# Plain fp32 products for every up-projection of a scan and mixture-of-experts kernel, in place of some products of high and low fp32r parts

## What is computed

```python
state = state * dA + (d_t * u_t)[..., None] * B_t[:, None, :]
y_t = jnp.einsum('ben,bn->be', state, C_t)
...
shared_out = jax.nn.silu(xf @ shared_wg.T) * (xf @ shared_wu.T) @ shared_wd.T
h = jax.nn.silu(jnp.einsum('td,efd->etf', xf, exp_wg)) * jnp.einsum('td,efd->etf', xf, exp_wu)
all_out = jnp.einsum('etf,edf->etd', h, exp_wd)
```

## Time and profile before

| | |
|---|---|
| median of 3 runs | 253.39 us (253.25 to 253.78) |
| the profiled execution's own time | 253.55 us |
| its span (first to last instruction) | 251.7 us |
| mean granted TensorE clock, share of full speed | 0.919 |
| matmul records on PE | 874 |

### The profile page before, as it was taken

One profiled execution on the slowest core, in us unless ns is written; L12 is line 12 of the kernel. 1 busy time (PEld: TensorE's weight loads), 2 busy tenths in 40 slices (PEclk: granted clock), 3 DMA queues, 4 the chain that ended last, 5 costly groups with the idle time before them and its releaser, 6 DMA issues. The chain is left out here.

```text
span 251.7 us, 3757 instructions
## 1 busy us (share of the span) xinstructions
PE 205.5 (82%) x874; PEld 148.7 (59%) x874; DVE 215.0 (85%) x522; ACT 171.2 (68%) x508; POOL 195.3 (78%) x237
## 2 busy tenths in 40 slices
PE   8534594658669895677996899889999999999995
PEld 4223273434355662345854587568888778788884
DVE  2789999999998989999999999989999999645340
ACT  4579879997758997458757998676775682343220
POOL 0248889999999999999999999999999996510000
PEclk9855579575979999999999999999999999999999
DMA  6496999770490202002209302020300000000000
GB/s 183 140 263 172 336 410 321 281 230 1 130 364 12 83 21 87 0 16 68 81 14 329 109 0 83 27 83 3 101 3 0 22 3 3 21 0 0 3 21 21
DMA packets 26821, 25.45 MB, mean 101 GB/s; under 512 B 1064, under 2 KB 25904, under 8 KB 26160
## 3 DMA queue, kind: packets, MB, share of 16 engines
q1 hardware_dynamic: 26512, 25.06, 30.7%
q10 hardware_dynamic: 288, 0.16, 0.2%
HBM read 24.04 MB, written 1.18 MB: 100 GB/s over the span
## 5 line engine op out<-in xcount | busy, mean ns | idle before, releaser
L1061 POOL TENSOR_TENSOR dbu<-du,bb 128x512 f32<-128x512 f32 x64 | 81.3, 1284 | 5.1 <-DVE du L463 3.3
L704 ACT ACTIVATE psA<-delta,aneg 128x127 f32<-128x127 f32 x256 | 78.0, 358 | 5.6 <-DVE psH L953 5.3
L953 DVE TENSOR_TENSOR_SCAN psH<-psA,dbu 128x512 f32<-128x512 f32 x64 | 76.5, 1218 | 1.5 <-POOL dbu L1087 0.4
L667 PE MATMUL psU<-wup,hnT 128*128 128x352 f32 x176 | 63.6, 491 | 12.8 <-DVE hcat L869 8.9
L1104 POOL TENSOR_TENSOR acc<-acc,prod 128x512 f32<-128x512 f32 x42 | 54.5, 1297 | 2.4 <-DVE prod L963 1.8
L545 PE MATMUL psD<-wdn,hT 128*128 128x256 f32 x224 | 52.2, 380 | 0.6 <-issue 0.6
L667 PEld LDWEIGHTS psU<-wup,hnT 128*128 128x128 f32 x176 | 32.8, 200 | 32.8 <-DVE hcat L869 13.6
L833 ACT ACTIVATE tg<-psU 128x176 f32<-128x176 f32 x80 | 24.4, 314 | 36.7 <-PE psU L667 23.9
L545 PEld LDWEIGHTS psD<-wdn,hT 128*128 128x128 f32 x224 | 41.5, 190 | 6.7 <-issue 1.1
L963 DVE TENSOR_TENSOR prod<-psH,cc 128x512 f32<-128x512 f32 x64 | 41.9, 679 | 1.1 <-POOL acc L1104 0.7
L1035 DVE SCALAR_TENSOR_TENSOR ag<-tg,psU 128x176 f32<-128x176 f32 x80 | 25.5, 330 | 15.5 <-ACT tg L833 15.1
(11 more groups left out here) (117 smaller groups left out, 282.9 us busy)
## 6 DMA issues: line engine op xcount, KB each, us to landing
cc<-brows SPq DMA_DIRECT2D x16, 512.0 KB, 4.9
bb<-brows SPq DMA_DIRECT2D x3, 2048.0 KB, 7.6
wup<-in_w_up SPq DMA_DIRECT2D x1, 1760.0 KB, 12.2
wdn<-in_w_down SPq DMA_DIRECT2D x1, 1664.0 KB, 16.5
wup<-in_w_up SPq DMA_DIRECT2D x1, 1408.0 KB, 8.4
x_sb<-in_x SPq DMA_DIRECT2D x4, 256.0 KB, 4.2
bb<-brows SPq DMA_DIRECT2D x1, 1024.0 KB, 5.9
out<-outb SPq DMA_DIRECT2D x8, 128.0 KB, 1.7
```

The source lines that it names most:

```text
L667: last = pe.matmul(dst, hnT[:, b % 2, k, lh * P:(lh + 1) * P], wup[:, j - 1, k, :], start=(k == 0), stop=(k == KT - 1))
L704: last = act.activation(dst[:, j, h, 1:], delta[:, b % 2, h, l0 + 1:l1], ACT.Exp, scale=aneg[:, h * DS + s0 + j:h * DS + s0 + j + 1])
L953: dve.tensor_tensor_scan(psH[:, i % 2], psA[:, i % DA_RING], dbu[:, i % DBU_RING], 0.0, ALU.mult, ALU.add).then_inc(s_scan, 1)
L1061: pool.tensor_tensor(tile(dbu[:, m % DBU_RING], m), du[:, b % 2, :, l0:l1].unsqueeze(1).broadcast_to(shape), bb[:, b % 2, s0:s0 + ns, l0:l ...
```

## The change

The table `SPLIT`, the four tiles of high and low parts, their four semaphores and the four tasks that make the parts are gone. Every unit but unit 0 of a tile goes through the plain branch. The lists of `ORDER` are other lists, found by a new search; each engine has the same tasks as before but the conversions. The arithmetic of the 28 units is now fp32 by fp32.

```diff
-SPLIT = ((1, 2), (3, 3), (5, 2), (7, 3), (9, 2))
...
-        whi = sb("whi", [P, NSPLIT, KT, 2 * FF], F32R)
-        wlo = sb("wlo", [P, NSPLIT, KT, 2 * FF], F32R)
...
-        hnhi = sb("hnhi", [P, 2, KT, P], F32R)
-        hnlo = sb("hnlo", [P, 2, KT, P], F32R)
...
-                    elif j not in SLOT or t < SPLIT[SLOT[j]][1]:
+                    else:
                         for k in range(KT):
                             last = pe.matmul(dst, hnT[:, b % 2, k, lh * P:(lh + 1) * P], wup[:, j - 1, k, :],
                                              start=(k == 0), stop=(k == KT - 1))
-                    else:
-                        slot = SLOT[j]
-                        if t == SPLIT[slot][1]:
-                            pe.wait_ge(s_wlo, CONVERT.index(slot) + 1)
-                        if j == next(q for q, first in SPLIT if first <= t):
-                            pe.wait_ge(s_hnlo, t - FIRST_SPLIT + 1)
-                        for k in range(KT):
-                            h_hi, h_lo = hnhi[:, t % 2, k, :], hnlo[:, t % 2, k, :]
-                            w_hi, w_lo = whi[:, slot, k, :], wlo[:, slot, k, :]
-                            pe.matmul(dst, h_hi, w_hi, start=(k == 0), stop=False)
-                            pe.matmul(dst, h_hi, w_lo, start=False, stop=False)
-                            last = pe.matmul(dst, h_lo, w_hi, start=False, stop=(k == KT - 1))
...
-                    act.copy(hnhi[:, i % 2], hnT[:, b % 2, :, h * P:(h + 1) * P]).then_inc(s_hnhi, 1)
...
-                    act.copy(whi[:, CONVERT[i]], wup[:, j - 1]).then_inc(s_whi, 1)
...
-                    pool.tensor_tensor(hnlo[:, i % 2], hnT[:, b % 2, :, h * P:(h + 1) * P], hnhi[:, i % 2],
-                                       ALU.subtract).then_inc(s_hnlo, 1)
...
-                    pool.tensor_tensor(wlo[:, k], wup[:, SPLIT[k][0] - 1], whi[:, k], ALU.subtract).then_inc(s_wlo, 1)
```

Of the lists, the lines of VectorE's that hold `route:4`:

```diff
-        mul:38 prod:48 gate:39 mul:39 keep_ends:48 prod:49 keep_ends:49 gate:40 route:4 mul:40 gate:41
...
+        mul:38 prod:48 gate:39 scan:49 mul:39 gate:40 route:4 mul:40 keep_ends:49 gate:41 mul:41 residual:5
```

More of the change, by code:

```diff
@@ L154 @@
[L154 to L157, removed]
+        project:0 project:1 xproj:0 dt:0 xproj:1 dt:1 project:2 prod:0 prod:1 prod:2 xproj:2 prod:3 prod:4
@@ L162 @@
[L162 to L176, removed]
@@ L191 @@
[L191 to L195, removed]
@@ new lines @@
+        z_gate:0 scan:5 delta2:1 keep_ends:4 keep_ends:5 prod:4 prod:5 scan:6 scan:7 prod:6 keep_ends:6
+        keep_ends:7 z_stats:3 prod:7 scan:8 log_1:2 gate_y:0 scan:9 residual:0 prod:8 stats:0 log_2:2 variance:0
+        scan:10 prod:9 prod:10 scan:11 scan:12 tap0:3 tap1:3 prod:11 tap2:3 scan:13 gate:0 route:0 mul:0 prod:12
+        prod:13 scan:14 scan:15 gate:1 gate:2 mul:1 mul:2 silu_u:3 prod:14 prod:15 scan:16 scan:17 prod:16
+        prod:17 keep_ends:16 gate:3 gate:4 keep_ends:17 mul:3 scan:18 mul:4 scan:19 gate:5 keep_ends:18
@@ new lines @@
+        prod:49 scan:50 scan:51 stats:5 keep_ends:50 gate:42 gate:43 variance:5 prod:50 keep_ends:51 mul:42
+        mul:43 scan:52 prod:51 prod:52 scan:53 gate:44 gate:45 prod:53 keep_ends:52 mul:44 mul:45 keep_ends:53
+        scan:54 finish:3 gate:46 mul:46 gate:47 mul:47 scan:55 prod:54 prod:55 gate:48 gate:49 mul:48
+        keep_ends:54 keep_ends:55 mul:49 z_gate:3 scan:56 scan:57 gate:50 gate:51 route:5 mul:50 mul:51 prod:56
+        prod:57 scan:58 gate:52 mul:52 scan:59 finish:4 gate:53 mul:53 gate:54 mul:54 residual:6 stats:6
@@ new lines @@
+        variance:6 gate:55 mul:55 gate:56 mul:56 prod:58 prod:59 gate:57 mul:57 scan:60 prod:60 gate:58 gate:59
+        mul:58 mul:59 scan:61 scan:62 prod:61 gate:60 prod:62 route:6 mul:60 gate:61 mul:61 scan:63 prod:63
+        gate:62 mul:62 gate:63 finish:5 mul:63 gate:64 mul:64 gate:65 residual:7 mul:65 stats:7 variance:7
+        gate:66 mul:66 gate:67 mul:67 gate:68 mul:68 gate:69 mul:69 route:7 gate:70 mul:70 gate:71 gate:72
+        mul:71 mul:72 gate:73 mul:73 gate:74 gate:75 mul:74 mul:75 gate:76 mul:76 finish:6 gate:77 gate:78
@@ L220 @@
+        mul:77 mul:78 gate:79 mul:79 finish:7
     """,
     "GpSimd": """
-        z_stats:0 z_stats:1 first:0 scan:0 scan:1 z_stats:2 z_stats:3 scan:2 scan:3 scan:4 scan:5 scan:6 scan:7
-        carry:0 weights_lo:0 scan:8 fix:8 fix:9 carry:1 scan:9 fix:10 scan:10 scan:11 fix:11 fix:12 weights_lo:1
-        variance:0 scan:12 prod:9 delta0:2 fix:13 prod:10 scan:13 scan:14 fix:14 fix:15 prod:11 delta1:2 prod:12
-        delta2:2 prod:13 scan:15 scan:16 scan:17 scan:18 prod:14 scan:19 prod:15 prod:17 scan:20 prod:18 scan:21
```

145 lines of the change are left out of this document (67 added, 78 removed).

## The result

The changed kernel takes 251.89 us in the median of 13 runs (251.35 to 253.12), the kernel before 253.39 us in the same session. The ratio is 0.9947 with a 95% interval of 0.9932 to 0.9962, so the change gains 1.3 us. The forecast was 255.6 us with a range of 252.7 to 258.5 us; both the sign and the range were wrong. The profiled execution of the changed kernel took 251.83 us, with a span of 250.0 us and 818 matmul records.

A forecast was written before the change was run, and what follows sets the result against it. The prediction took DVE's arrival at `route:4` plus PE's work from there as the bound: 253.55 + 4.4 - 0.8 - 1.4 = 255.75 us, as a median 255.6 us, range 252.7 to 258.5 us.

The forecast's parts named there:

- What bounds the kernel: End of kernel: the moment DVE reaches `route:4` and the first product behind it, plus PE's remaining work.
- PE pays 19 x 0.23 = 4.4 us: PE after the hand-over: 19 split units become plain, each 0.23 us longer, 4.4 us on the path.
- POOL's shorter list, 1.4 us: Before 162 us: POOL's shorter list gives back DVE's waits for POOL, 1.4 us, between bounds of nothing and 7.3 us.
- The ACT conversions: ACT: removing conversions of 3.8 and 2.4 us is worth nothing by itself.
- The lists, 0.8 us: DVE ahead of `route:4`: one product and one small copy move behind it, 0.8 us earlier; other moves cost nothing.
- The bound on DVE's idle time: DVE from 20 us to the hand-over: at most 149.1 - 141.8 = 7.3 us of idle time can be given back.
- the 1 to 3 us named as a sign: Changed profile, 20 us to the hand-over: DVE's idle time falls by 1 to 3 us.
- the first, faster: Up to `route:4`: POOL is the real pacemaker; 5.5 us of DVE idle time given back makes 251.5 us; chance 0.11.
- The even case: Ahead of `route:4`: the lists win back waits of 3.4 us, time 253.6 us; chance 0.13.
- the two slower ones: Forecast's case, PE's 4.4 us paid, 254.0 to 257.0 us, chance 0.63; and the third rival, chance 0.13.
- the third rival: Before the hand-over: PE becomes the bound, 26 units each 0.23 us longer, 258.6 us; chance 0.13.
- The checks named at the end of the prediction: Wrong if `route:4` is done before 164.5 or after 169 us, or the last stretch is not 4 to 5 us longer.

The follow-up runs named there:

- The two runs in old lists: Kernel before, old lists, conversions out: plain products 254.18 us (ratio 1.0037); fp32r products of a blank tile 250.62 us (0.9897).
- the cuts: Plain, no conversions: new lists to tile 4, then old 254.38 us; opposite 254.85 us; new to tile 2 257.56 us; cut behind hand-over 253.01 us.

## Why the prediction was wrong, by its own steps

**What bounds the kernel** was read rightly: the time is the hand-over at `route:4` plus PE's work from there. In the traces of all eleven kernels with plain products throughout, the stretch from `route:4` to the end of the span lasts 86.3 to 87.4 us; what sets them apart lies ahead of it.

**PE pays 19 x 0.23 = 4.4 us**: right in mechanism, somewhat large. The two runs in old lists give 3.5 us. In their traces the chain's pieces behind `route:4` show why. In the kernel before, the 19 split units take 18.9 us and the 16 plain ones (units 0 of a tile apart) 19.8 us, 0.99 and 1.24 us each; with plain products throughout the 35 take 42.2 us, 1.21 each. 42.2 - 38.7 is 3.5 us. The single unit I read the earlier trace rows was one without a wait; on average split units gave some of their advantage back in waits, and so did the plain units between them. The rule of the Trainium skill ("TensorE: Matmul & The Clock Gate", Back-to-back issue gap, with "FP8 and Floating Point Precision") gives an estimate of 5.7 us, further off.

**POOL's shorter list, 1.4 us**: too small. Taking out the conversions was worth 2.6 us in the old lists. DVE's idle time up to `route:4` did fall by just 1.4 us (14.1 to 12.7 us), but its busy time fell by 0.8 us too, and the hand-over came 2.2 us earlier. That part is no shorter work: counts times mean durations of DVE's rows up to `route:4` add up to 177.5 us before and 177.8 us without the conversions, so its instructions only follow each other with more overlap. Rows of waits did not show that. The step also had "POOL can come to tile 4's statistics about ten us earlier": it came 3.3 us earlier with the old lists and 7.6 us with the new ones. That DVE is late next was right, with PE beside it. The ACT conversions, costed at nothing, are in the 2.6 us as well; no run takes those out alone, so their share stays open.

**The lists, 0.8 us**: this is the step that failed most, and with it the sign. The new lists were worth 2.3 us. The prediction compared which tasks stand ahead of `route:4` on DVE, found two that moved, and priced them by their length. That price was about right for these two: put back, they cost 0.9 us at `route:4`, and 1.3 to 1.6 us in all. What failed is that the order of the tasks that stay ahead of `route:4` was priced at nothing. It gives a lead of some 1.3 us by `route:3`, where none of the moved tasks has been reached. Which moves make that lead was not found; the cuts only show that it is lost easily. Another 0.95 us is made between `route:3` and `route:4`, where the moved tasks of all three engines stand. On ACT the prediction looked at the conversions alone, and costed them at nothing because ACT was busy 23.91 of 29.08 us. `z_norm:3`, `scan:48` and `z_gate:3` go behind `norm:4`, and directly ahead of it they cost 2.1 us. A busy share does not tell whether an engine's queue stands ahead of the one task that is waited for. In the kernel before, though, ACT was idle for 1.63 us until POOL's `nb` came: its order began to matter only when POOL was early. The three prices need not add up; the runs do not put them together.

**The bound on DVE's idle time** was sound: of the 7.3 us from 20 us on 3.3 us were given back, a little over the 1 to 3 us named as a sign, and 0.8 us lost again ahead of 20 us. But it was a bound on idle time only. DVE's busy time up to `route:4` fell from 154.7 to 151.9 us. By counts times mean durations 1.7 us of this is shorter work, 0.8 us of it the two moved tasks and 0.65 us the product `sz` (below); the other 1.1 us is more overlap between instructions. That was in none of the terms.

**The rival** whose result came true is the first, faster, with a chance of 0.11. Its mechanism, POOL as pacemaker, is only half right: with POOL shortened and the lists kept, the kernel is slower than before, and its condition, 4.1 us of DVE's idle time given back, was not met (3.3 us). "DVE's list can be put together with more freedom when POOL is early" is the part of it that held. The even case and the two slower ones fall by their times, but a part of the third rival's mechanism shows: from 144.88 to 155.82 us the changed kernel's chain is on PE.

The checks named at the end of the prediction: `route:4` done before 164.5 us (it was 163.49 us) was one of the signs of error, and it said that DVE's order was not tight. POOL at 183.1 us of busy time came as written, DVE's was 213.0 us where near 215 us had been, and the last stretch from unit 42's product to PE's last matmul is 247.37 - 163.78 = 83.6 us, where "some 84 us" had been written (before 79.9 us, so 3.7 us longer and not 4 to 5).

## What to carry to other kernels

When several engines meet at one hand-over, look on each of them for what stands in its queue directly ahead of the task that the next engine waits for, and for which of them comes last; a busy share or a sum of work ahead does not price it. The set of tasks ahead of a point is not their order: here a search that nearly kept the set moved the point by over 2 us. Taking 12.8 us of work out of a full engine was worth 2.6 us in the order made around that work, and putting it into the order made without it cost 10.1 us, so a removal and a new order have to be costed together. A cheaper instruction that needs preparation pays where the preparing engines have idle time and no hand-over waits for them: here six units of the last tile gave 1.1 of the 1.2 us expected.

## What the runs showed of the hardware

DVE's product `sz`, whose two inputs both lie in SBUF (`zt` and `zn`), takes 667 to 700 ns in most places and up to 1.67 us in others. Before, changed, and new lists with conversions (min, median and max ns of 4):

```profile
L979 DVE SCALAR_TENSOR_TENSOR sz<-zt,zn x4: 667/788/1124, 31.9 to 187.4; 128x512 f32<-128x512 f32 x4
```

```profile
L944 DVE SCALAR_TENSOR_TENSOR sz<-zt,zn x4: 671/676/827, 30.5 to 182.5; 128x512 f32<-128x512 f32 x4
```

```profile
L980 DVE SCALAR_TENSOR_TENSOR sz<-zt,zn x4: 671/757/1634, 30.1 to 191.5; 128x512 f32<-128x512 f32 x4
```

What decides is which of the two engines was first. In the third kernel POOL's sum `acc`, also with both inputs in SBUF, had begun 0.18 us earlier, and `sz` is long:

```profile
84.49 1.26 POOL L1105 TENSOR_TENSOR acc<-acc,prod 128x512 f32<-128x512 f32 x1
...
84.67 1.63 DVE L980 SCALAR_TENSOR_TENSOR sz<-zt,zn 128x512 f32<-128x512 f32 x1
```

Over fifteen traces, four `sz` each, a `dbu` or `acc` of 128x512 was under way on POOL 35 times when `sz` began. In the 21 cases in which more than 0.12 us of it was left, `sz` took 0.67 us and what was left, less 0.12 us, to within 0.02 us: here 0.67 + 1.08 - 0.12 = 1.63 us. In the other 14 it took its 0.67 to 0.68 us. Where `sz` began first, an `acc` that began beside it took longer: at 187.53 us of the kernel before 1.72 us, where the median is 1.28 us. "SBUF — State Buffer" of the Trainium skill, Who interferes with whom, says that a DVE instruction with two SBUF inputs contends with a GpSimd instruction that reads SBUF, and that one with at most one, outside DVE's 2-port modes, does not. The traces agree: most other DVE instructions in these lists read PSUM for one input and kept their mean within 14 ns. Over the three `sz` before 163 us the mean is 890 ns before and 674 ns in the changed kernel, 0.65 us of the 2.8 us by which DVE's busy time to `route:4` fell. So the length of such a DVE instruction hangs on when POOL's starts and not only on how much POOL has to do.

An fp32r product of 352 columns is spaced at 0.16 us, a plain fp32 unit at 1.18 to 1.19 us for four records, at the same granted clock of 1.00 (2.4 GHz). Six of the one make 0.96 us, so three fp32r products in place of one fp32 product save a fifth, if nothing waits and their parts cost nothing.
